# A causal attention layer on one core: its probabilities are exchanged in pieces, with two buffers each way, in place of a head at a time

## What is computed

```python
q = (xn @ wq.T).reshape(B, S, 16, 192)            # 128 nope + 64 rotary
kv = xn @ wkv_a.T                                  # 128 latent + 64 rotary key
kv_cache = rmsnorm(kv_lat, kv_norm_w)
q_lat = einsum('bshd,hdc->bshc', q_nope, wkv_b_h[:, :128])
scores = (q_lat . kv_cache + q_pe . k_pe) * SCALE  # causal mask
attn = softmax(scores)
out_lat = einsum('bsht,btc->bshc', attn, kv_cache)
out = (out_lat through wkv_b_h[:, 128:]) @ wo.T    # 16 heads
ffn = xn @ ternary(weight).T + bias
```

## Time and profile before

| | us |
|---|---|
| median of 3 runs | 2135.69 (2128.77 to 2140.19) |
| the profiled execution, its own time | 2143.6 |
| its span, first to last instruction | 2141.6 |
| TensorE busy | 1793.0 (84%) |
| VectorE busy | 1214.6 (57%) |
| GpSimd busy | 1003.5 (47%) |
| ScalarE busy | 851.5 (40%) |
| granted TensorE clock, mean | 0.915 of full |

### The profile page before, as it was taken

How to read it: one execution, slowest core, us unless ns; L and a number is a source line. 1 busy time by engine, 2 the same in 40 slices (tenths; PEclk the granted TensorE clock), 3 DMA queues, 4 the chain that set the end, 5 groups by cost and what they waited for, 6 DMA issues and landing times.

```text
span 2141.6 us, 25543 instructions
## 1 busy us (share of the span) xinstructions
PE 1793.0 (84%) x8174; PEld 1455.8 (68%) x8174; DVE 1214.6 (57%) x2769; ACT 851.5 (40%) x1326; POOL 1003.5 (47%) x634
## 2 busy tenths in 40 slices
PE   6997888787889889778878787888899889898985
PEld 5785677576777667656656576676677667776764
DVE  5764567565666666445455454556555655564652
ACT  4553444333544443333433333333444343434332
POOL 4763445324554554344434444434444454545445
PEclk9888999998999999898989898899999999999988
DMA  6992555646556564553544445455465445644544
GB/s 226 355 312 95 152 151 164 192 112 167 157 134 155 155 181 124 148 136 96 133 117 112 130 112 135 147 133 153 121 152 136 126 116 133 162 111 118 141 115 108
DMA packets 127171, 317.33 MB, mean 148 GB/s; under 512 B 29442, under 2 KB 41987, under 8 KB 125508
## 3 DMA queue, kind: packets, MB, share of 16 engines
q1 hardware_dynamic: 126224, 314.62, 53.4%
q10 hardware_dynamic: 820, 1.15, 0.2%
HBM read 113.28 MB, written 34.60 MB: 69 GB/s over the span
## 4 chain that ended last, share of the span: by engine, by line
issue 24%; PE 23%; SPq 16%; POOL 15%; DVE 7%; ACT 3%; DMA 3%; POOLq 0%; DVEq 0%; ACTq 0%
SPq L943 16%; POOL pT L1312 10%; PE p_out L1075 10%; PE p_score L1057 9%; DVE turned L1145 3%; DMA pT<-turned 2%; POOL qp_l L1301 2%; POOL qp_l L1298 2%; PE p_lat L1037 2%; PE p_result L1087 1%; ACT qp_h L1258 1%; PE p_rot L1037 1%; DVE probs L1122 1%; ACT probs L1225 1%; DVE q_l L1168 1%
## 5 line engine op out<-in xcount | busy, mean ns | idle before, releaser
L1312 POOL TENSOR_TENSOR pT<-pT,pT_h 128x1024 fp32r<-128x1024 f32 x320 | 683.7, 2162 | 484.6 <-ACT pT_h L1237 480.6
L1122 DVE TENSOR_SCALAR_CACHE_REDUCE probs<-p_score 128x512 f32<-128x512 f32 (+3 forms) x640 | 382.0, 602 | 488.2 <-PE p_score L1057 338.6
L1225 ACT ACTIVATE probs<-probs,neg_max 128x128 f32<-128x128 f32 (+15 forms) x256 | 306.9, 1199 | 513.6 <-DVE neg_max L1128 513.3
L1145 DVE STREAM_TRANSPOSE turned<-probs 128x1024 f32<-128x1024 f32 (+7 forms) x384 | 341.8, 915 | 219.6 <-DMA pT<-turned 196.7
L1237 ACT ACTIVATE pT_h<-pT 128x1024 fp32r<-128x1024 f32 x320 | 299.4, 966 | 260.0 <-PE p_out L1075 172.6
L1057 PE MATMUL p_score<-Kn_h,q_h 128*128 128x512 f32 (+3 forms) x640 | 253.9, 397 | 110.5 <-DVE q_l L1168 67.1
L1075 PE MATMUL p_out<-pT_h,V_h 128*128 128x512 f32 (+3 forms) x640 | 256.8, 401 | 57.0 <-POOL pT L1312 56.9
L1087 PE MATMUL p_result<-Wv,o_h 128*128 128x512 f32 x512 | 171.4, 417 | 122.4 <-DVE acc L1187 111.9
L1057 PE MATMUL p_score<-Kp,qp_h 128*128 128x512 f32 (+3 forms) x640 | 244.8, 382 | 10.5 <-POOL qp_l L1301 9.9
L1075 PE MATMUL p_out<-pT_h,V_l 128*128 128x512 f32 (+3 forms) x640 | 248.2, 388 | 0.0
L1075 PE MATMUL p_out<-pT,V_h 128*128 128x512 f32 (+3 forms) x640 | 247.7, 387 | 0.0
(11 more groups left out here) (135 smaller groups left out, 2614.5 us busy)
## 6 DMA issues: line engine op xcount, KB each, us to landing
pT<-turned SPq DMA_DIRECT2D x768, 128.0 KB, 2.3
pT<-turned SPq DMA_DIRECT2D x512, 96.0 KB, 2.1
Wq<-wq_scr SPq DMA_DIRECT2D x63, 512.0 KB, 3.5
Wv<-wv_scr SPq DMA_DIRECT2D x63, 512.0 KB, 4.2
pT<-turned SPq DMA_DIRECT2D x256, 64.0 KB, 2.0
Wp<-wp_scr SPq DMA_DIRECT2D x31, 512.0 KB, 4.4
xT_scr<-xT SPq DMA_DIRECT2D x3, 2048.0 KB, 10.1
xT<-xT_scr SPq DMA_DIRECT2D x3, 2048.0 KB, 10.9
```

The source lines that it names most:

```text
L1122: dve.tensor_scalar(probs[row % ROW_RING][:, b * CW:b * CW + width], p_score[n % SCORE_RING][:, 0:width], SCALE, LOWEST, ALU.mult, ALU.max ...
L1145: last = dve.transpose(to.rearrange("p a t q -> p t a q"), rows.rearrange("p (t a q) -> p t a q", a=4, q=32))
L1225: act.activation(probs[row % ROW_RING][:, 0:width], probs[row % ROW_RING][:, 0:width], ACT.Exp, bias=neg_max[p][:, i:i + 1], scale=1.0, ac ...
L1312: pool.tensor_tensor(low, low.bitcast(F32), high.bitcast(F32), ALU.subtract).then_inc(p_low, 1)
```

## The change

The unit of the order is no longer a head but a slot (slot(s) in place of step(g)). In chunks 0 and 1 a slot is a head. In chunks 2 and 3 it is half a head, two of its four rows, so there are 2 x 16 + 4 x 16 = 96 slots (SLOTS). What a slot makes is a piece. turned and pT become two buffers each, of half the size: the same memory. A piece of two rows and up to 16 tiles fills one.

- A piece is exchanged in one go of 16 DMAs; a head of chunks 2 and 3 still has 32. VectorE waits, before the first row of piece s, for the exchange of piece s - 2 only, and SyncE for the values of piece s - 2.
- A group is still 1024 columns: four tiles by two rows in chunks 2 and 3. The value matmuls of these chunks have at most 256 columns, into half of p_out, and there are 22 tile steps a head in chunk 2 (36 value matmuls become 66) and 30 in chunk 3 (48 become 90).
- p_out is split piece by piece, half as wide each (high_output, split_output twice a head).
- The order in each slot is new (high_place, split_place, value_unit, out_heads, out_unit). The output projection comes up to a slot later, and inv_sum has four buffers.
- The Wq load moves from SyncE's queue to ScalarE's (load_q in the block of act); the Wv load stands in the middle of an exchange in chunk 0 and behind it later, the Wp load in the middle.

```diff
+GROUP = 1024
...
+def head_of(s):
+    return s if s < 2 * H else H + s // 2
+def piece_of(g, i):
+    return g if g < 2 * H else 2 * (g - H) + i // 2
+def last_piece(g):
+    return piece_of(g, QB - 1)
+def rows_of(s):
+    return QB if s < 2 * H else QB // 2
+def first_row(s):
+    return 0 if s < 2 * H else 2 * (s % 2)
+def opens_head(s):
+    return s < SLOTS and first_row(s) == 0
+def closes_head(s):
+    return first_row(s) + rows_of(s) == QB
+def piece_tiles(s):
+    return QB * chunk_of(head_of(s)) + first_row(s) + rows_of(s)
+def group_tiles(s, k):
+    wide = GROUP // (P * rows_of(s))
+    return wide * k, min(wide * (k + 1), piece_tiles(s))
...
+def phase(s):
+    return chunk_of(head_of(min(s, SLOTS - 1)))
+def units_of(s):
+    return rows_of(s) * (phase(s) + 1)
+def unit_of_head(s, u):
+    return first_row(s) * (phase(s) + 1) + u
+def value_unit(s, k):
+    return (2 + k, 1 + k, 2 + k, 1 + 2 * k)[phase(s)]
+def split_place(s):
+    last = value_unit(s + 2, groups_of(s) - 1)
+    return (s + 2, last + 1) if last + 1 < units_of(s + 2) else (s + 3, 0)
+def high_place(s, k):
+    if k < HIGH_RING:
+        return (s + 2, 0) if phase(s + 1) in (0, 2) else (s + 1, units_of(s + 1) - 1)
+    return s + 2, value_unit(s + 2, k - HIGH_RING)
+def out_heads(s):
+    if s < H:
+        return (s - 3,) if s >= 3 else ()
+    if s < 2 * H:
+        return (s - 3, s - 2) if s == H else (s - 2,)
+    if s == 2 * H + 1:
+        return (2 * H - 2,)
+    return (s // 2 + H - 2,) if s % 2 == 0 and s > 2 * H else ()
+def out_unit(s, g, i):
+    if s < H:
+        return 1
+    if s < 2 * H:
+        return 0 if g == s - 3 else 6 + i // 2
+    return 2 + i if s % 2 == 0 else i
+def latent_unit(s, it):
+    if s < 2 * H:
+        return (1 + it // 2, 2 + it)[phase(s)]
+    return (it if phase(s) == 2 else 1 + it) if s < SLOTS and closes_head(s) else None
+def query_unit(s):
+    if s < 2 * H:
+        return (3, 6)[phase(s)]
+    return (4 if phase(s) == 2 else 5) if s < SLOTS and closes_head(s) else None
+def rotate_ops(s, u):
+    if phase(s) == 0:
+        return ((), (0, 1, 2), (3, 4), ())[u]
+    return ((0,), (1, 2), (3, 4))[u - 1] if 1 <= u <= 3 else ()
+def rotary_add_unit(s):
+    return (2 if phase(s) == 0 else 4) if opens_head(s) else None
+def rotary_high_unit(s):
+    return (3 if phase(s) == 0 else 5) if opens_head(s) else None
...
-        turned = sb("turned", [P, 4, NT, QB, 32])
-        pT = sb("pT", [P, 4, NT, QB, 32], F32R)
-        pT_h = [sb(f"pT_h{i}", [P, 4, 2, QB, 32], F32R) for i in range(HIGH_RING)]
+        turned = [sb(f"turned{i}", [P, NT * QB * P // 2]) for i in range(2)]
+        pT = [sb(f"pT{i}", [P, NT * QB * P // 2], F32R) for i in range(2)]
+        pT_h = [sb(f"pT_h{i}", [P, GROUP], F32R) for i in range(HIGH_RING)]
...
-            def exchange(g, part):
-                first, end = part_tiles(g, part)
-                tiles = slice(tile_base(g) + first, tile_base(g) + end)
-                sp.wait_ge(blocked, QB * (g + 1))
-                need(sp, pv_done, free_by(g, end))
-                for a in range(4):
+            def exchange(s, quarters):
+                g, tiles = head_of(s), piece_tiles(s)
+                sp.wait_ge(blocked, QB * g + first_row(s) + rows_of(s))
+                need(sp, pv_done, groups_before(s - 1) if s >= 1 else 0)
+                for a in quarters:
                     for r in range(4):
-                        sp.dma_start(pT[32 * a:32 * (a + 1), r, tiles, :, :].bitcast(F32),
-                                     turned[32 * r:32 * (r + 1), a, tiles, :, :]
-                                     ).then_inc(exchanged[part][g % 2], 16)
-            def load_q(g):
-                sp.wait_ge(lat_projected, g)
-                sp.dma_start(Wq[:, :, :, :].bitcast(F32), t["wq_scr"][g % H]).then_inc(wq_in, 16)
+                        sp.dma_start(slots(pT[s % 2][32 * a:32 * (a + 1), :], s)[:, r, 0:tiles, :, :].bitcast(F32),
+                                     slots(turned[s % 2][32 * r:32 * (r + 1), :], s)[:, a, 0:tiles, :, :]
+                                     ).then_inc(exchanged[s % 2], 16)
...
+            def slot(s):
+                if 1 <= s <= SLOTS:
+                    exchange(s - 1, (0, 1))
+                if opens_head(s) and head_of(s) % 2 and head_of(s) + 3 < HEADS:
+                    load_rotary(head_of(s) + 3)
+                if s < H:
+                    load_next_v(s)
+                if 1 <= s <= SLOTS:
+                    exchange(s - 1, (2, 3))
+                if s >= H:
+                    load_next_v(s)
+                if s < SLOTS and closes_head(s):
...
+            def load_next_v(s):
+                for g in out_heads(s):
+                    if g + 1 < HEADS:
+                        load_v(g + 1)
...
+                if i == first_row(s) and s >= 2:
+                    dve.wait_ge(exchanged[s % 2], 256 * (s // 2))
...
+            def high_group(s, k):
+                n = groups_before(s) + k
+                if k == 0:
+                    act.wait_ge(exchanged[s % 2], 256 * (s // 2 + 1))
+                need(act, pv_done, n - HIGH_RING + 1)
...
+            def load_q(g):
+                act.wait_ge(lat_projected, g)
+                act.dma_start(Wq[:, :, :, :].bitcast(F32), t["wq_scr"][g % H]).then_inc(wq_in, 16)
...
```

More of the change, by code:

```diff
@@ L54 @@
 HIGH_RING = 3
+GROUP = 1024
 HEADS = NCH * H
+SLOTS = 2 * H + 4 * H
 def need(eng, sem, value):
@@ new lines, in first_row, with groups_of, groups_before @@
+def first_row(s):
[9 more added lines that the diff above has]
+    return wide * k, min(wide * (k + 1), piece_tiles(s))
+def groups_of(s):
+    return -(-piece_tiles(s) * rows_of(s) * P // GROUP)
+def groups_before(s):
+    return sum(groups_of(i) for i in range(s))
@@ L899, in build_attention @@
         wv_in = sem("wv_in")
-        exchanged = [[sem(f"exchanged{part}{i}") for i in range(2)] for part in range(2)]
+        exchanged = [sem(f"exchanged{i}") for i in range(2)]
         result_out = sem("result_out")
@@ L1005, in _ @@
             sp.wait_ge(stored["acc"], 16 * (NCH - 1))
-            load_q(1)
             load_rotary(2)
-            for g in range(HEADS + 2):
-                step(g)
+            for s in range(SLOTS + 3):
+                slot(s)
             store_chunk(NCH - 1)
@@ L1062, in scores, with values @@
                 mm.then_inc(scored, 1)
[L1064 to L1065 removed]
+            def values(s, k):
+                g, n = head_of(s), groups_before(s) + k
                 if k == 0:
[L1068 to L1076 removed]
+                    need(pe, o_split, s)
+                pe.wait_ge(p_low, n + 1)
+                first, end = group_tiles(s, k)
+                out = result_columns(p_out, s)
+                for t in range(first, end):
+                    i = max(0, t - QB * chunk_of(g) - first_row(s))
+                    cols, rest = slice(i, rows_of(s)), slice(i - rows_of(s), None)
+                    low, high = group(s, k)
+                    for a, (v, pt) in enumerate(((V_h, high), (V_l, high), (V_h, low))):
+                        mm = pe.matmul(out[:, :, cols, :], v[:, t, :], pt[:, :, t - first, rest, :],
+                                       start=(t == 0 and a == 0), stop=(t == piece_tiles(s) - 1 and a == 2))
                 mm.then_inc(pv_done, 1)
@@ L1212, in _ @@
+                    for i in range(rows_of(s) - 1 if s < SLOTS else 0):
+                        if u == row_unit(s, i):
+                            turn_row(g, first_row(s) + i)
             for op in range(5):
```

293 lines of the change are left out of this document (116 added, 177 removed).

## The result

| | before | changed |
|---|---|---|
| median of 14 runs each, us | 2135.18 (2127.45 to 2140.19) | 2122.43 (2115.17 to 2129.33) |
| ratio, 95% interval | | 0.9947 [0.9931, 0.9963] |
| span of the profiled execution | 2141.6 | 2113.1 |
| TensorE busy | 1793.0 | 1803.1 |
| granted clock, mean | 0.915 | 0.92 |

The change is 0.5% faster; the forecast was 1969 us with a range from 1905, so the sign was right and the size was not, and the result lies outside the range. The same reciprocals as in the earlier trace rows, changed kernel: count, durations, first and last start in each chunk.

A forecast was written before the change was run, and what follows sets the result against it. Circles of waits, a different longest one in each chunk, were taken to bound the kernel: 2143.6 - 14 - 48 - 90 - 6 - 9 = 1976.6 us profiled, less 7.9 for the median, gives 1969 us, range 1905 to 2045.

The forecast's parts named there:

- An exchange of a piece stays at 12.1: All chunks: 16 DMA issues to last landing take 12.1 us, as before, since an issue lasts the same for any size.
- Chunk 3, 41.6 us: Head time in chunk 3: a one-slot circle through landing, ScalarE, VectorE and exchange, 20.8 us twice; gain -6 us.
- ends 2 us before: Chunk 3: TensorE's path ends 2 us before the third group's ring slot is wanted, so it adds nothing.
- Chunk 2, 31.5 us: Head time in chunk 2: a two-slot circle through the exchange, 30.1 us, plus ScalarE lateness and clock; gain -90 us.
- up to 0.6 late: Chunk 2: ScalarE, in the slot's last exponential, takes the group up to 0.6 us late, making 30.1 into 30.7.
- Chunk 1, 20.3 us: Head time in chunk 1: query rounded ahead of the groups, waits go, TensorE's 19.1 plus 1.2 remain; gain -48 us.
- Chunk 0, 14.1 us: Head time in chunk 0: ScalarE's exchange circle is cut, TensorE's 11.9 plus query and small waits remain; gain -14 us.
- The changes of chunk: nothing, same loads.: Transitions between chunks: no gain or loss, 0 us, because the loads are the same.
- End: After the last row, four groups pass GpSimd rather than eight, 2.38 us each: -9 us.
- Narrow matmuls do not overlap: Rival, value loops of chunks 2 and 3: each 256-column value matmul takes its 0.28 us; 2155 us in all, chance 5%.
- The clock falls in every slot: Rival, chunks 2 and 3: TensorE's idle stretches each cost 1.5 us through a slower clock; 2038 us in all, chance 17%.
- TensorE bounds: Rival: circles are slacker than added up, chunk 2 at 27.6 and chunk 3 at 34.9 us; 1814 us in all, chance 7%.

The follow-up runs named there:

- experiment 2: Changed kernel with the Wq load back in SyncE's queue and Wq, Wp and Wv all behind the whole exchange: 2042.04 us.
- Experiment 6: Changed kernel, loads unrepaired, with chunk 3's first three groups of a piece rounded at unit 0 of the slot after: 2101.18 us.
- experiment 8: Kernel of experiment 2 with chunk 2's values one unit later (3, 4, 5 in place of 2, 3, 4): 2001.25 us.
- experiment 3: Changed kernel with only the Wp and Wv loads behind the whole exchange, Wq still on ScalarE's queue: 2062.65 us.
- experiment 1: Changed kernel with only the Wq load moved back to SyncE's queue, behind the whole exchange: 2082.99 us.
- experiment 12: Changed kernel with loads behind exchanges, later groups and values in chunks 2 and 3, chunk 0's output projection at unit 3, Wq ahead of Wv there: 1876.45 us.

## Why the prediction was wrong

Two steps failed: the size of an exchange, and the circle that I took to bound chunk 2.

**"An exchange of a piece stays at 12.1"** is the first, with the loads costed at little or nothing beside it: the Wq load "went to ScalarE's queue, which has idle time", and of Wp and Wv in the middle there was only "now and then a Wp load among the issues", priced by its issue. I priced a load by what its issue costs its queue and not by what its bytes do to the DMA engines. From the first issue to the last landing, the mean in the changed kernel is 15.9, 14.4, 13.0 and 13.6 us in the four chunks; with all loads behind it is 12.0, 12.6, 12.0 and 12.2. I had the earlier trace rows with a DMA share of 0.47 for a chunk and did not open a window on a single exchange; before, one such window reads 0.92 (208 GB/s).

Of the 139 us by which the forecast change (-167) missed the measured one (-28), this is 60 by the spans of the profiled executions, and 80 by the medians: the execution profiled for experiment 2 is 13 us above its median, the changed kernel's 7 below. What is left with all loads behind lies in chunk 0 (26 us), chunk 2 (26), chunk 1 (20) and the changes of chunk (7). That the sign came out right is partly luck: chunks 1 and 2 gained 57 us, and chunks 0 and 3 and the changes of chunk gave back 41.

**Chunk 3, 41.6 us.** Mechanism and size right, once the landings are: 41.8 with the loads behind. The changed kernel has 43.8. Here a slot has no slack, so each late landing is paid at once. Whether TensorE's path "ends 2 us before" in this order was not measured. Experiment 6 shows only that the circle which its own order makes lies directly below, so the cut of one circle alone gave little.

**Chunk 2, 31.5 us.** Measured 34.8; 33.7 with the loads behind. TensorE's wait for GpSimd has the size that I gave it, 57.4 us from 850 to 1340 us in the changed kernel, about 2 in each of some 28 slots. But the circle behind it is another, and this is the second step that failed. Mine went through an exchange, which was 12.1 of its 30.1 us. The chain of the changed kernel from 870 to 1340 us holds no issue and no transfer of an exchange, and from 870 to 1250 ScalarE waited for a landing 5 times, 11.9 us in all. One round of what the chain does hold (start us, us, what):

```profile
1103.41 0.76 PE p_result L1133 x3
...
1105.31 0.64 ACT qp_h L1310
1106.01 1.31 POOL qp_l L1356
1107.39 1.31 POOL qp_l L1359
1108.84 2.37 POOL pT L1367
1111.35 2.80 PE p_out L1121 x12
```

After the last output projection come the roundings of half an output and of the rotary halves, GpSimd's two rotary subtractions, and only then the group that the values wait for: the circle of one slot that the expectation of experiment 8 names. I had priced ScalarE at the slot's end as "up to 0.6 late" and left GpSimd's rotary work out. Experiment 8 moves the half output out of this path and takes 3.1 us off a head. With that the forecast circle appears to come next: ScalarE then waits for a landing 25 times, 42.8 us, from 850 to 1290 us. So that the 13 distances ahead of the wait for the next chunk's x (below) are 32.8 us on average with the loads behind, only 1.3 over the forecast, is luck. A sum was off as well: 24% of a head of 37.9 us is 9.1 us, and not 9.7. Why Wp and Wv behind the exchange gain 16 us in this chunk (experiment 3) and Wq none was not taken apart.

**Chunk 1, 20.3 us.** The wait of the earlier trace rows is gone, as said. In the steady part the kernel with the loads behind has 20.65, mean of the first 13 distances. Most of the rest of the missing gain is the 14th distance, 34.8 us, where I had used 20.3 for all of them. Before, the long distance at the end of the chunk (31.2) is the 15th, outside the 14 that I counted.

**Chunk 0, 14.1 us.** Right that the old circle is cut and the query is next; its price was short. The late landings are not the cause: experiments 1 and 2 made them earlier and the chunk no shorter (207.4 and 209.9 us for 203.4). The chain shows what I left out: GpSimd's rotary addition of 1.30 ahead of the two roundings in every second head. And TensorE's waits came out as reckoned (21.4 us over 13 heads, 1.6 each, in experiment 2), but the granted clock there is 0.90, and the 957 matmuls recorded from 206 to 462 us are 208.9 us busy, where experiment 12, at 0.95, has the same number in 193.0.

**"The changes of chunk: nothing, same loads."** +9. TensorE's first rotary projection of a chunk waits for x: 28.8 us over three chunks, before 14.9 over two. The 2 MB load of x was issued at 1326.64 and landed at 1335.16, and the projection starts at 1335.25:

```profile
1335.25 5.27 PE L1081 MATMUL p_rot<-xT,Wp 128*128 128x512 f32 x12 [7.82 <-issue]
```

**End**: -13 for -9, right in kind.

**The rivals.** *Narrow matmuls do not overlap* is refuted. Value matmuls of 256 columns, in chunk 3 of the changed kernel, first in one slot, then after a wait in another:

```profile
1785.00 0.28 PE L1121 MATMUL p_out<-pT,V_h 128*128 128x256 f32 x1
1785.12 0.28 PE L1121 MATMUL p_out<-pT_h,V_h 128*128 128x256 f32 x1
...
1796.49 0.58 PE L1121 MATMUL p_out<-pT_h,V_h 128*128 128x256 f32 x1 [4.60 <-DVE o_l L1219]
1796.87 0.41 PE L1121 MATMUL p_out<-pT_h,V_l 128*128 128x256 f32 x1
1797.08 0.41 PE L1121 MATMUL p_out<-pT,V_h 128*128 128x256 f32 x1
```

They stand 0.12 apart in the first slot and 0.21 in the second, after an idle of 4.60 us. The windows on the two slots tell the granted clock (the figure ahead of the last two):

```profile
1784.00:1787.00 3.00, 3.00 (x21) 2.71 (x20) 3.00 (x6) 1.25 (x2) 1.58 (x2) 1.00 1.03 243
1796.40:1799.40 3.00, 2.91 (x13) 2.91 (x14) 2.66 (x5) 0.00 (x0) 2.73 (x2) 0.50 0.03 5
```

1.00 and 0.50, so 2.4 and 1.2 GHz: the spacing follows the clock, and at the full one it is what I took. *The clock falls in every slot* is real, then, and small: chunks 2 and 3 have 0.92, with the loads behind 0.94, and there chunk 3 keeps to 41.8, not to the 44.6 of that rival. *TensorE bounds* named a floor of 27.6 and 34.9 us in chunks 2 and 3. Experiment 12 has 30.6 and 35.8, so chunk 3 comes within 1 us of it and chunk 2 within 3, but only a rearrangement that this change doesn't have gets that near. The true case, a bulk load that delays an exchange, was not among my rivals, although the change moved three loads.

## What to carry to other kernels

Price a DMA that is moved twice: the issue on its queue, and its bytes against the transfers in flight, read from a window on one of them and not from a chunk's average. In a circle of waits the last landing sets the time, so bulk loads go behind the last piece of a latency-bound exchange, and ahead of anything that waits longer than they do. Where one circle is cut, work out the next one down before forecasting the gain: in chunk 3 the first cut alone brought 0.9 us of 43.8. And a wait of the forecast size does not prove the forecast circle: follow the chain behind it, as in chunk 2.

## What was unexpected of the hardware

- In the two exchanges read above (128 KB every 0.63 us), a load of 512 KB delays all later transfers by about 2 us, until the exchange's end, whichever of the two queues it came from; a load of 128 KB left no such delay in the means. The Wq load was itself in flight from 1405.43 to 1412.71 us, while the last transfer was issued at 1409.98. The Wp load had landed at 1431.54, yet the transfer issued at 1431.98 still took 4.26 us; whether that is what Wp left behind or the Wv load, issued at 1432.62, is open.
- The loads' costs don't add: 39, 60, and together 80 us.
